# A column scan with its two halves interleaved on three engines, and Fourier passes cut into two column halves

## The reference

```python
def _cell(prev_col, cur_col, weight_ih, bias_ih, weight_hh, bias_hh):
    C = cur_col.shape[-1]
    pad = jnp.pad(prev_col, ((0, 0), (1, 1), (0, 0)))
    x = jnp.concatenate([pad[:, :-2], pad[:, 1:-1], pad[:, 2:]], axis=-1)
    i_vals = jnp.einsum('bhk,ok->bho', x, weight_ih) + bias_ih
    h_vals = jnp.einsum('bhc,oc->bho', cur_col, weight_hh) + bias_hh
    r_i, z_i, n_i = jnp.split(i_vals, 3, axis=-1)
    r_h, z_h, n_h = jnp.split(h_vals, 3, axis=-1)
    r = jax.nn.sigmoid(r_i + r_h)
    z = jax.nn.sigmoid(z_i + z_h)
    n = jnp.tanh(n_i + r * n_h)
    return n * z + cur_col * (1.0 - z)
...
x = x + _L0_conv_ref(_gn(x), L0_conv_weight, L0_conv_bias)
x = x + _L1_conv_ref(_gn(x), L1_conv_weight_ih, L1_conv_bias_ih, L1_conv_weight_hh, L1_conv_bias_hh)
x = x + _L2_conv_ref(_gn(x), L2_conv_w_real, L2_conv_w_imag)      # rfft2, 16x16 modes times weights, irfft2
x = x + _L3_conv_ref(_gn(x), L3_conv_kernel_re, L3_conv_kernel_im, L3_conv_bias)   # rfft2, all modes, irfft2
```

## Time and profile before

| | |
|---|---|
| median of three runs (lowest to highest) | 596.94 (596.35 to 597.09) |
| the profiled execution: time, span | 597.76, 595.9 |
| mean granted TensorE clock | 0.988 of full speed |
| busy in the span: PE, DVE, ACT, POOL | 539.8, 492.0, 396.7, 311.3 |
| the scan | about 117 to 322 |
| forward transform, spectral layers, backward | about 323 to 403, 403 to 513, 513 to 595 |

### The profile page before, as it was taken

One profiled execution on the slowest core, in us unless ns is written; L12 is line 12 of the kernel. 1 busy time (PEld: TensorE's weight loads), 2 busy tenths in 40 slices (PEclk: granted clock), 3 DMA queues, 4 the chain that ended last, 5 costly groups with the idle time before them and its releaser, 6 DMA issues.

```text
span 595.9 us, 26842 instructions
## 1 busy us (share of the span) xinstructions
PE 539.8 (91%) x10404; PEld 429.0 (72%) x10404; DVE 492.0 (83%) x1273; ACT 396.7 (67%) x897; POOL 311.3 (52%) x425
## 2 busy tenths in 40 slices
PE   3999999699999999999999999988889778999996
PEld 2333333477777777777777999987577667899995
DVE  7778977479989898989898787798899999377876
ACT  3445879767777776777778966676378966756441
POOL 7665654156666666666665302035799799121000
PEclk9999999899999999999999999999999997999999
DMA  6900000011111111111113100003158775003324
GB/s 226 383 6 0 2 2 4 14 39 44 40 40 44 38 41 44 36 44 40 40 44 103 50 2 0 0 2 85 60 151 248 213 227 158 31 1 142 141 123 159
DMA packets 21284, 45.69 MB, mean 77 GB/s; under 512 B 5104, under 2 KB 15600, under 8 KB 20352
## 3 DMA queue, kind: packets, MB, share of 16 engines
q1 hardware_dynamic: 20160, 44.97, 24.2%
q10 hardware_dynamic: 672, 0.15, 0.1%
q0 software_dynamic: 416, 0.07, 0.1%
HBM read 28.53 MB, written 8.39 MB: 62 GB/s over the span
## 4 chain that ended last, share of the span: by engine, by line
DVE 40%; PE 36%; issue 14%; ACT 6%; DVEq 2%; DMA 1%; SPq 0%; ACTq 0%
PE psum L655 8%; DVE spec L1352 8%; DVE work L338 7%; DVE spec L1344 6%; DVE spec L1355 5%; PE psum L770 5%; PE psum L909 5%; PE psum L925 5%; PE psum L786 4%; DVE small L1237 3%; PE psum L898 3%; PE psum L754 2%; ACT work L295 2%; PE psum L828 2%; DVE spec L1347 2%
## 5 line engine op out<-in xcount | busy, mean ns | idle before, releaser
L690 PE MATMUL psum<-spec,matrices 128*32 128x128 f32 x3024 | 110.0, 279 | 14.4 <-ACT spec L1016 7.5
L690 PEld LDWEIGHTS psum<-spec,matrices 128*32 128x32 f32 x3024 | 76.5, 110 | 46.6 <-ACT spec L1016 46.5
L531 POOL TENSOR_TENSOR spec<-spec 64x128 f32<-64x128 f32 x126 | 70.6, 560 | 72.1 <-DVE spec L1355 72.1
L697 PE MATMUL psum<-spec,matrices 128*32 128x128 f32 x3024 | 107.4, 274 | 0.7 <-DMA spec<-work 0.6
L697 PEld LDWEIGHTS psum<-spec,matrices 128*32 128x32 f32 x3024 | 85.6, 111 | 3.7 <-issue 3.6
L828 PE MATMUL psum<-work 128*32 128x128 f32 x2368 | 74.8, 281 | 14.8 <-ACT work L350 10.2
L655 PE MATMUL psum<-spec,matrices 128*64 128x512 f32 x384 | 86.4, 607 | 1.1 <-ACT spec L950 1.1
L828 PEld LDWEIGHTS psum<-work 128*32 128x32 f32 x2368 | 65.7, 113 | 23.7 <-issue 22.2
L338 DVE TENSOR_TENSOR work<-spec,psum 32x512 f32<-32x512 f32 x108 | 73.5, 681 | 3.8 <-PE psum L828 0.5
L509 POOL TENSOR_SCALAR spec<-image,small 32x960 f32<-32x960 f32 (+1 forms) x48 | 55.5, 1157 | 34.6 <-PE psum L655 22.0
L525 POOL TENSOR_TENSOR image<-image,spec 128x128 f32 (+1 forms) x128 | 69.4, 542 | 0.0
(11 more groups left out here) (154 smaller groups left out, 935.5 us busy)
## 6 DMA issues: line engine op xcount, KB each, us to landing
work<-w_dram SPq DMA_DIRECT2D x33, 512.0 KB, 4.2
spec<-work SPq DMA_DIRECT2D x124, 64.0 KB, 1.9
image<-x_dram SPq DMA_DIRECT2D x3, 2048.0 KB, 11.7
out_dram<-image SPq DMA_DIRECT2D x3, 2048.0 KB, 6.3
image<-x_dram SPq DMA_DIRECT2D x4, 512.0 KB, 5.8
work<-w_dram SPq DMA_DIRECT2D x1, 2048.0 KB, 7.7
out_dram<-image SPq DMA_DIRECT2D x4, 512.0 KB, 2.9
kept<-const_dram SPq DMA_DIRECT2D x1, 192.0 KB, 5.5
```

The lines of the kernel that those rows point to most:

```text
L531: nc.gpsimd.tensor_tensor(straddled(h, ROWS_01, 0), *of, ALU.subtract).then_inc(lower_ready[h], 1)
L690: last = mm(psum[QUARTERS[hm], 4 * h + g, 0:HB], sv[:, g, QUARTERS[hm]], moving[hm], start=starts, stop=True)
L697: last = mm(psum[q, 4 * h + g, 0:HB], sv[:, 3 + g, q], e, start=True, stop=stops)
```

## The change

The scan is written in another order on three engines, and four lines of matmuls are cut in two.

- DVE: the reset product of half 1 now stands ahead of the state of half 0.
- ACT: the copy of half 1's state stands ahead of half 0's update gate.
- PE: after the first step, both halves' first column passes come first, and the other two of half 1 stand between the state passes of half 0. Each pass waits for its own bank, not for all three.
- `in_two`, and the loop in `over_h`: each full pass of ih, iw, fw and fh becomes two with 64 of the stationary's columns each, on two halves of the array, with the same moving operand. Transposes and sums stay whole.

The names h_sum, r_sum, n_sum and z_sum in what follows are the semaphores of PE's passes; r_gate, z_gate and n_gate those of ACT; reset_done, pre_ready, keep_ready, mix_ready and state_ready those of DVE; lower_ready and added those of POOL; sedge_ready that of ACT's copy. The last digit is the half. L1344, L1347, L1352, L1355, L1360 become L1367, L1372, L1377, L1380, L1387.

```diff
--- before.py
+++ after.py
@@ -626,6 +626,12 @@
                 for _ in range(n):
                     mm(psum[:, 4, 0:P], data, data, start=True, stop=True)
 
+            def in_two(out, stationary, moving):
+
+                for o in (slice(0, P // 2), slice(P // 2, P)):
+                    last = mm(out[o], stationary[:, o], moving, start=True, stop=True)
+                return last
+
             def sum0_of(lo, n, need):
 
                 pe.wait_ge(stat0, need)
@@ -697,36 +703,53 @@
                     last = mm(psum[q, 4 * h + g, 0:HB], sv[:, 3 + g, q], e, start=True, stop=stops)
                 return last
 
-            def half_step(h, w, parity, nth):
-                if nth is None:
-                    pe.wait_ge(cur_first[h], 32)
-                else:
-                    pe.wait_ge(cur_in[parity], nth * 32)
-                    pe.wait_ge(r_gate[h], w - 1)
-                    pe.wait_ge(z_gate[h], w - 1)
-                    pe.wait_ge(reset_done[h], w - 1)
-                from_column(h, 0, parity)
-                from_column(h, 1, parity)
-                from_column(h, 3, parity, True).then_inc(h_sum[h], 1)
+            def half_step(h, w):
+                pe.wait_ge(cur_first[h], 32)
+                from_column(h, 0, w % 2)
+                from_column(h, 1, w % 2)
+                from_column(h, 3, w % 2, True).then_inc(h_sum[h], 1)
                 pe.wait_ge(sedge_ready[h], w)
                 pe.wait_ge(lower_ready[h], w)
                 from_state(h, 0).then_inc(r_sum[h], 1)
                 from_state(h, 2, True).then_inc(n_sum[h], 1)
                 from_state(h, 1).then_inc(z_sum[h], 1)
 
+            def step(w, parity, nth):
+
+                pe.wait_ge(cur_in[parity], nth * 32)
+                for h in range(2):
+                    pe.wait_ge(r_gate[h], w - 1)
+                    from_column(h, 0, parity)
+                pe.wait_ge(z_gate[0], w - 1)
+                from_column(0, 1, parity)
+                pe.wait_ge(reset_done[0], w - 1)
+                from_column(0, 3, parity, True).then_inc(h_sum[0], 1)
+                pe.wait_ge(sedge_ready[0], w)
+                pe.wait_ge(lower_ready[0], w)
+                from_state(0, 0).then_inc(r_sum[0], 1)
+                from_state(0, 2, True).then_inc(n_sum[0], 1)
+                pe.wait_ge(z_gate[1], w - 1)
+                from_column(1, 1, parity)
+                from_state(0, 1).then_inc(z_sum[0], 1)
+                pe.wait_ge(reset_done[1], w - 1)
+                from_column(1, 3, parity, True).then_inc(h_sum[1], 1)
+                pe.wait_ge(sedge_ready[1], w)
+                pe.wait_ge(lower_ready[1], w)
+                from_state(1, 0).then_inc(r_sum[1], 1)
+                from_state(1, 2, True).then_inc(n_sum[1], 1)
+                from_state(1, 1).then_inc(z_sum[1], 1)
+
             pe.wait_ge(scan_w_in, 16 * 14)
             pe.wait_ge(bias_written, 2)
             pe.wait_ge(conv_added, 2 * B)
-            half_step(0, 1, 1, None)
+            half_step(0, 1)
             pe.wait_ge(stat1, (NG - 1) * KGN + steps_all(GB - 1) + steps_all(1))
-            half_step(1, 1, 1, None)
+            half_step(1, 1)
             with pe.Fori(0, (W - 4) // 4) as i:
                 for k in range(4):
-                    for h in range(2):
-                        half_step(h, i * 4 + (k + 2), k % 2, i * 2 + (k // 2 + 1))
+                    step(i * 4 + (k + 2), k % 2, i * 2 + (k // 2 + 1))
             for w in (W - 2, W - 1):
-                for h in range(2):
-                    half_step(h, w, w % 2, w // 2)
+                step(w, w % 2, w // 2)
 
 
             bw = by_w.rearrange("p (c m e) -> p m c e", m=P, e=2)
@@ -767,9 +790,8 @@
                         pe.wait_ge(w_act, j * 12 + 2 * (k - 3))
                         pe.wait_ge(w_dve, j * 12 + 2 * (k - 3))
                     for c in range(6 * k, min(6 * k + 6, C)):
-                        last = mm(psum[:, (c // 3 + 4) % 8, 4 * PADK * (c % 3):4 * PADK * (c % 3) + 4 * PADK],
-                                  bw[:, :, c // 2, c % 2], cm["fw"],
-                                  start=True, stop=True)
+                        last = in_two(psum[:, (c // 3 + 4) % 8, 4 * PADK * (c % 3):4 * PADK * (c % 3) + 4 * PADK],
+                                      bw[:, :, c // 2, c % 2], cm["fw"])
                     last.then_inc(w_done, 1)
 
             def over_h(j, last_group=False):
@@ -783,8 +805,10 @@
                         else:
                             pe.wait_ge(t_act, j * 6 + (7 + BY_ACT.index(n)))
                     for b in range(GB):
-                        last = mm(psum[:, n, 2 * H * b:2 * H * b + 2 * H], bh[:, b, n % 2, 4 * (n // 2):4 * (n // 2) + 4], cm["fh"],
-                                  start=True, stop=True)
+                        k4, e = 4 * (n // 2), n % 2
+                        for i, half in enumerate((slice(k4, k4 + 2), slice(k4 + 2, k4 + 4))):
+                            last = mm(psum[P // 2 * i:P // 2 * (i + 1), n, 2 * H * b:2 * H * b + 2 * H], bh[:, b, e, half],
+                                      cm["fh"], start=True, stop=True)
                     last.then_inc(h_done, 1)
                 if last_group:
                     pe.wait_ge(h_act, j * 6 + 2)
@@ -906,8 +930,7 @@
                     if not first:
                         pe.wait_ge(image_done, j * 16 + (2 * n - 14))
                     for i in range(4):
-                        last = mm(psum[:, n, P * i:P * i + P], kh[:, :, 2 * n + i // 2, i % 2], cm["ih"],
-                                  start=True, stop=True)
+                        last = in_two(psum[:, n, P * i:P * i + P], kh[:, :, 2 * n + i // 2, i % 2], cm["ih"])
                     last.then_inc(b_done, 1)
                 if not last_group:
                     back_transposes(j + 1, False)
@@ -922,7 +945,7 @@
                     for i in range(2):
                         for x_ in range(2):
                             at_ = 256 * i + 128 * x_
-                            last = mm(psum[:, n, at_:at_ + 128], kwv[:, x_, n, i], cm["iw"], start=True, stop=True)
+                            last = in_two(psum[:, n, at_:at_ + 128], kwv[:, x_, n, i], cm["iw"])
                     last.then_inc(c_done, 1)
 
             back_transposes(0, True)
@@ -1030,8 +1053,8 @@
 
             def scan_step(w):
                 reset_gate(0, w)
+                state_edges(1, w - 1)
                 update_gate(0, w)
-                state_edges(1, w - 1)
                 candidate(0, w)
                 reset_gate(1, w)
                 update_gate(1, w)
@@ -1338,10 +1361,12 @@
                     dve.wait_ge(columns_ready, B)
                 v.tensor_copy(state[h], columns[:, h * HB:h * HB + HB]).then_inc(state_ready[h], 1)
 
-            def new_state(h, w):
+            def reset_product(h, w):
                 dve.wait_ge(r_gate[h], w)
                 dve.wait_ge(h_sum[h], w)
                 v.tensor_tensor(pre1[h], gr[h], psum[:, 4 * h + 3, 0:HB], ALU.mult).then_inc(reset_done[h], 1)
+
+            def mixed(h, w):
                 dve.wait_ge(reset_done[h], w)
                 dve.wait_ge(n_sum[h], w)
                 v.scalar_tensor_tensor(out=pre2[h], in0=psum[:, 4 * h + 2, 0:HB], scalar=bias_s[:, 2:3], in1=pre1[h],
@@ -1353,16 +1378,25 @@
                                        op0=ALU.subtract, op1=ALU.mult).then_inc(keep_ready[h], 1)
                 dve.wait_ge(n_gate[h], w)
                 v.tensor_tensor(mix[h], gn[h], gz[h], ALU.mult).then_inc(mix_ready[h], 1)
+
+            def new_state(h, w):
                 dve.wait_ge(mix_ready[h], w)
                 dve.wait_ge(keep_ready[h], w)
                 dve.wait_ge(added[h], w)
                 dve.wait_ge(sedge_ready[h], w)
                 v.tensor_tensor(state[h], mix[h], keep[h], ALU.subtract).then_inc(state_ready[h], 1)
 
+            def step(w):
+                reset_product(0, w)
+                mixed(0, w)
+                reset_product(1, w)
+                new_state(0, w)
+                mixed(1, w)
+                new_state(1, w)
+
             with dve.Fori(0, (W - 1) // 3) as i:
                 for k in range(3):
-                    for h in range(2):
-                        new_state(h, i * 3 + (k + 1))
+                    step(i * 3 + (k + 1))
 
 
             dve.wait_ge(added[0], W)
```

## The result

The changed kernel takes 601.78 us (601.56 to 601.86), the kernel before 597.02 in the same comparison (596.35 to 598.07): a ratio of 1.0081, interval 1.0068 to 1.0094. It is slower by 4.8 us, where +3.2 had been forecast. The profiled execution after took 601.7, its span is 599.8.

What follows compares the result with a forecast made beforehand. No single bound: DVE sets the pace in the scan, PE in the Fourier stages. 597.76 us of the profiled execution + 8.1 (scan) - 4.9 (halves) = 601.0, or 600.2 from the median; range 590 to 607.

Steps and rivals of the forecast that it cites:

- The hold: Scan: POOL's subtract starts 0.14 us ahead of state(0) and keeps it out, so state ends 0.15 after the subtract.
- X: Scan: time from mix(0) to the end of state(0), 0.80 us undisturbed, 0.97 if POOL's subtract holds state.
- the branch: DVE's scan loop goes round every third step, adding 0.38 us there; steps of 3.25 become 3.6.
- rival A: Scan: state(0) gets in before POOL's subtract, step 3.19 us, total 589.5; chance 0.19.
- The scan's total: Scan: mean step 3.36 us against 3.23, +0.13 over 62 steps, +8.1 us.
- PE's order: Scan: PE's new order of passes costs nothing by itself; without ACT's cover a late pass would cost 0.22 us a step.
- The halves: Fourier stages: full passes cut into two column halves go at 0.109 us a pair instead of 0.118; net -4.9 us.
- the 14 changes: Fourier stages: 14 more changes between full array and halves, 0.1 us each, 1.4 us.
- C: Fourier stages: cut passes stay at 0.118 us and only the array changes cost, total 606.4 us; chance 0.04.
- D: Fourier stages: half passes are bound by their loads, 0.139 us a pair, total 626 us; chance 0.03.
- From sum to median: Whole kernel: the profiled execution lay 0.8 us above the median, so the sum of 601.0 became 600.2.
- ring: Scan: closed chain of waits through both halves on ACT and DVE, 2.26 us plus state(0)'s part 0.97, 3.23 a step.

Runs made afterwards that it cites:

- Short subtract: The changed kernel with POOL's straddle subtract of half 0 cut from 128 columns to 16, waits and queues unchanged: 587.52 us.

## Why the prediction was right, and where its sizes were off

- **The hold** was the step on which the sign rested, and it held: state(0) 0.50 to 0.57 with its end 0.14 after the subtract's, state(1) 0.29. Predicted X = 0.97, measured 0.96 (245.22 to 246.18); predicted steps 3.25 and 3.6 at the branch, mean 3.36; measured 3.21, 3.25, 3.63, mean 3.367. Short subtract shows it as the cause. The lead was 0.10 in this step and 0.03 in the step after a branch, not 0.14, and state(0) was held in both. The Trainium skill, "SBUF — State Buffer", section Who interferes with whom, says that issue order decides; these rows agree.
- **The rival A** was mis-sized: with the hold away it is 587.5, not 589.5, because X alone is 0.75, not 0.80. The term was above all the 0.30 from mix to reset product, which is 0.26.
- **The scan's total** was forecast at 8.1, 0.13 x 62. By the measured step it is 0.138 x 62 = 8.6, and the scan ends 8.9 later. Of the other 0.3, 0.2 lies in the first three steps (13.08 against 11.70, less three times 0.138 and an earlier start of 0.76). There PE is granted half its clock (the 1.2 GHz level), after a stretch in which it was busy 0.86 of 4.00 us. In these windows of after (start and end, length, busy time and count of PE, PEld, DVE, ACT, POOL, granted clock, DMA share, GB/s)

```profile
113.00:117.00 4.00, 0.86 (x24) 0.59 (x24) 0.50 (x2) 3.92 (x6) 1.59 (x4) 0.88 0.07 16
117.00:122.00 5.00, 4.69 (x89) 4.72 (x93) 2.67 (x10) 1.73 (x7) 1.51 (x3) 0.50 0.23 56
122.00:330.00 208.00, 192.27 (x5922) 154.36 (x5912) 172.09 (x616) 137.11 (x494) 136.54 (x247) 1.00 0.16 38
```

  the clock is 0.50 from 117 to 122 us; before it was 0.61 there. Whether the clock makes the 0.2 was not tried.
- **PE's order** at nothing was right for this change alone, because ACT's copy stands ahead of the gate: without that it costs 11.5 us. The prediction's 0.22 a step for it would be 13.6.
- **The halves**: -4.9 forecast, -4.75 by stages (forward 1.36, backward 3.39). The total is better than its terms. Of the 14 changes two stand behind a wait and cost nothing; the other 12 cost 9 x 0.15 + 3 x 0.2 = 1.95, not 1.4, so the passes gave some 6.7, not 6.3, and the two misses cancel. C and D are out: pairs go at 0.109, over_w's at 0.116. The rule named beside D (the Trainium skill, "TensorEngine Tiling (Array Packing)", section Restrictions: column tiling disables fast weight load) shows no price here: a half's load takes 138 to 139 ns a record, where a full pass of the same line took 196. Whether the full passes' loads were fast ones, no run shows.
- **From sum to median**: the profiled executions differ by 3.9, the medians by 4.8, since the execution before lay 0.74 above its median and the one after at its own. This is half of the 1.6 by which the forecast fell short; the scan's 0.8 and the halves' 0.15, less the 0.24 of the spectral layers, make the rest. Without the 0.8 taken off, the forecast would have been 601.0, nearer to the result, but by the luck of one execution. In the spectral layers that execution was granted a clock of 0.50 from 493.0 to 499.8 us, the one after from 501.7 to 505.1 only, so their 0.24 is not put down to the change.

## What to carry to other kernels

Moving an instruction of one engine can change who reads first on another: before moving a DVE instruction with two operands in SBUF (the on-chip buffer in which `spec` and `work` lie), set its new start beside the POOL instructions that read SBUF, and in the estimate let the one that starts later wait for the end of the other. In this scan the two engines together fill most of a step, and an added wait only moved the hold to another DVE instruction; a subtract cut to 16 columns removed it (one that is as short and still fills the whole buffer was not tried). Single parts of a reordering need not add up: three of +10.0, +11.5 and +2.2 us made +9.4 together, so price the order of all queues at once, by its ring.

## What the runs showed of the hardware

- A DVE instruction that waits behind one POOL instruction is not next in turn: the following POOL instruction went first, and keep took 0.90 instead of 0.28.
- A lead of 0.03 us by the records was enough for POOL: state(0) took 0.57 instead of 0.29, with its end 0.15 after the subtract's.
- Full passes whose stationary lies with a stride went at 0.118; cut into two column halves, with the same strides, pairs go at 0.109, the pace of the transposes. The load records are 196 ns in those full passes, 138 to 139 in the halves and 140 in the transposes of L754. That the load sets the pace was not tried, and the transposes of L898, three groups with loads of 194 ns, went at 0.113.
- A change between full array and halves costs some 0.15, at the change itself (0.20 to 0.22 from start to start instead of 0.11 to 0.12) and at the next start (0.163 to 0.169 instead of 0.109 to 0.116); into the transposes of L922 it costs 0.2.
